# Attention block on one core: another order of the first batch's loads and value tiles, and output products of the last batch per head group

## What is computed

```python
h = jnp.maximum(_layernorm(x, axis=-1), 0.0)
q = heads(h @ Wq + bq); k = heads(h @ Wk + bk); v = heads(h @ Wv + bv)   # 16 heads of 32
scores = jnp.einsum('bhqd,bhkd->bhqk', q, k) * scale
scores = jnp.where(adj[:, None] == 0, -jnp.inf, scores)
attn = jax.nn.softmax(scores, axis=-1)
out = jnp.einsum('bhqk,bhkd->bhqd', attn, v)     # then the heads side by side again
return x + out @ Wo + bo
```

## Time and profile before

| | us |
|---|---|
| three runs: median (lowest to highest) | 1763.75 (1763.15 to 1766.16) |
| the profiled execution, its own time | 1761.98 |
| its span in the profile | 1760.2 |
| PE busy | 1695.4 (96%) |
| DVE busy, ACT busy | 1445.1, 1445.0 (82% each) |
| POOL busy | 139.8 (8%) |
| granted clock of PE, mean | 0.996 |

### The profile page before, as it was taken

The page is one execution under the profiler, slowest core; times in us unless marked ns, Lnnn a source line. Parts: engine busy times, 40 slices in busy tenths (PEclk is TensorE's granted clock), DMA queues, the critical chain, the costliest instruction groups (busy, mean ns, idle before and its releaser), DMA issues.

```text
span 1760.2 us, 27571 instructions
## 1 busy us (share of the span) xinstructions
PE 1695.4 (96%) x8129; PEld 1038.8 (59%) x8256; DVE 1445.1 (82%) x3493; ACT 1445.0 (82%) x3397; POOL 139.8 (8%) x200
## 2 busy tenths in 40 slices
PE   3989999999999999999999999999999999999997
PEld 2646666666666666666665666666566566666643
DVE  5778888888888888888888888888888888888783
...
DMA packets 118677, 175.18 MB, mean 100 GB/s; under 512 B 32384, under 2 KB 34432, under 8 KB 118528
## 3 DMA queue, kind: packets, MB, share of 16 engines
...
...
## 4 chain that ended last, share of the span: by engine, by line
PE 89%; DVE 5%; ACT 3%; issue 1%; DMA 1%; SPq 0%; POOL 0%; POOLq 0%; DVEq 0%; ACTq 0%
PE ps L666 16%; PE psP L590 14%; PE psO L697 14%; PE psP L592 13%; PE psP L591 13%; PE ps L677 12%; PE ps L680 5%; PE ps L638 2%; DVE ps L488 2%; ACT ps L349 1%; PE ps L644 1%; DVE x_tile L416 1%; DVE probs L495 1%; DVE oT_lo L508 1%; ACT probs L379 1%
## 5 line engine op out<-in xcount | busy, mean ns | idle before, releaser
L488 DVE CUSTOM_DVE_ANT_0 ps<-ps,bias_q 128x512 f32<-128x512 f32 x1024 | 710.7, 695 | 237.3 <-PE ps L666 223.4
L349 ACT ACTIVATE ps<-ps,neg_max 128x512 f32<-128x512 f32 x1024 | 680.9, 665 | 76.8 <-DVE neg_max L488 43.7
L379 ACT ACTIVATE probs<-ps 128x512 f32<-128x512 f32 x1024 | 613.2, 599 | 123.9 <-PE ps L677 100.3
L666 PE MATMUL ps<-k_stack,q_stack 96*128 96x512 f32 x1024 | 447.7, 437 | 12.6 <-ACT ps L349 9.4
L677 PE MATMUL ps<-q_stack,k_stack 98*128 98x512 f32 x1024 | 408.6, 400 | 4.0 <-ACT probs L379 3.3
L495 DVE SCALAR_TENSOR_TENSOR probs<-bias_k,probs 128x512 f32<-128x512 bf16 x512 | 365.4, 714 | 13.1 <-ACT probs L379 13.1
L666 PEld LDWEIGHTS ps<-k_stack,q_stack 96*128 96x128 f32 x1024 | 192.4, 188 | 257.8 <-ACT ps L349 108.6
L697 PE MATMUL psO<-probs,v_sb 128*32 128x512 f32 x2048 | 273.2, 605 | 2.7 <-DVE probs L495 1.5
L677 PEld LDWEIGHTS ps<-q_stack,k_stack 98*128 98x128 f32 x1024 | 194.8, 190 | 43.0 <-ACT probs L379 14.7
L349 ACT ACTIVATION_READ_ACCUMULATOR ps<-ps,neg_max 128x1 f32 x1024 | 208.5, 204 | 0.0
L680 PE MATMUL ps<-bias_k,ident_b 128*128 128x512 bf16 x385 | 150.7, 391 | 0.0
...
## 6 DMA issues: line engine op xcount, KB each, us to landing
q_stack<-part_hi SPq DMA_DIRECT2D x512, 64.0 KB, 2.0
k_stack<-part_hi SPq DMA_DIRECT2D x512, 64.0 KB, 2.0
...
```

Source lines behind the costliest of these rows:

```text
L349: nc.scalar.activation(item, item, ACT.Exp, scale=-1.0, bias=neg_max[:, g % 2, col:col + 1], accum_out=exp_sum[:, g % 2, col:col + 1]).the ...
L379: nc.scalar.activation(probs[:, n % P_RING, :], ps2[:, n % 2, :], ACT.Exp, scale=SCALE).then_inc(exp2_done, 1)
L488: nc.vector.tensor_tensor_reduce(bank1(("s", u)), bank1(("s", u)), bias_q[:, qt, :], -SCALE, 3.0e38, ALU.add, ALU.min, neg_max[:, g % 2, c ...
L666: nc.tensor.matmul(bank1(("s", u)), q_stack[0:STACK, g, j, P * qt:P * qt + P], k_stack[0:STACK, g, j, :], start=True, stop=True).then_inc( ...
```

## The change

- **Start.** SP issues x0, x1, then Wv in four quarters, then x2 and x3 (into `y_tile`, which is free), then the three bias vectors as rows into `c_rows`, then Wq, Wk, bo, and Wo after the low part of Wq. The empty block -1 is gone. Wv is staged in `v_sb` and split by quarters (`split_wv`); Wq is split at slots 9 (ACT) and 12 (DVE), Wk at 14 and 15, Wo at 25 and 26.
- **Value tiles.** In block 0 the tiles follow `FIRST_TILES`: v0, v1 and v2 stand in tiles 1 to 3, each waiting only for its own h tile, and v3 in the old place of v0. Tiles 9, 12 and 13 are empty.
- **Biases.** PE turns the three bias vectors in slot 2 of block 0 and ACT copies them to `cols`. PE waits there until they have landed. Before, three transfers of 4-byte elements brought them as columns.
- **Ones.** The two rows of ones in `k_stack` are written by POOL after the four `rstd` of batch 0, no longer by DVE as its first instruction.
- **End.** In blocks 16 and 17 `project_last(g)` makes, for head group g, the 12 products of all four output tiles, into four banks that are held from slot 36 on: g = 0 at slot 36, 1 at slot 42, 2 at slot 52 of block 16, and 3 at slot 0 of block 17. The first waits for the end of the first pass. Tiles 2 and 3 of y of batch 15 lie in `x_tile` and are loaded in slots 48 and 50, with no wait for a store.
- **In every block.** The bfloat16 identity (`ident_b`) is no tile of its own any more, but the upper halves of the float32 one, read with a step of two elements. `exp_sum` has one place in place of two, `ln_sum` is gone (its value goes to `c_all`), and ACT waits at the first exp of each group for the logarithm of the last.

```diff
+FIRST_TILES = [None, ("v", 0), ("v", 1), ("v", 2), ("q", 0), ("k", 0), ("v", 3), ("q", 1), ("k", 1), None, ("q", 2),
+               ("k", 2), None, None, ("q", 3), ("k", 3)]
 QKV_TILES = [x for x in TILES if x[0] != "o"]
+FIRST_QKV_TILES = [x for x in FIRST_TILES if x]
...
+LAST_OUT_AT = {36: 0, 42: 1, 52: 2}
...
-        bq_col = sb("bq_col", [P, NT], F32)
-        bk_col = sb("bk_col", [P, NT], F32)
-        bv_col = sb("bv_col", [P, NT], F32)
+        cols = sb("cols", [P, 3 * NT + 1], F32)
+        bq_col, bk_col, bv_col = (cols[:, NT * i:NT * i + NT] for i in range(3))
+        minus_half = cols[:, 3 * NT:3 * NT + 1]
...
-        ident_b = sb("ident_b", [P, P], BF16)
-        minus_half = sb("minus_half", [P, 1], F32)
+        ident_b = ident[:].bitcast(BF16).rearrange("p (q two) -> p q two", two=2)[:, :, 1]
...
-        exp_sum = sb("exp_sum", [P, 2, 16], F32)
-        ln_sum = sb("ln_sum", [P, 16], F32)
+        exp_sum = sb("exp_sum", [P, 16], F32)
...
+        w_staged = {"q": probs[:, 0:4, :], "k": probs[:, 4:8, :], "v": v_sb[:, 1, :, :], "o": probs[:, 0:4, :]}
+        LAST = B - 1
+        last_turn_bank = RING.index(("c", 3, -1)) % 3
+        last_out = [psP[:, 0, :], psP[:, 1, :]] + [ps1[:, i, :] for i in range(3) if i != last_turn_bank]
...
+        def x_view(b, t):
+            return (y_tile if b == 0 and t >= 2 else x_tile)[:, t % 2, :]
...
+        def y_view(b, t):
+            return (x_tile if b == LAST and t >= 2 else y_tile)[:, t % 2, :]
...
+        def tile_at(k, T):
+
+            if k == 0:
+                return FIRST_TILES[T] and FIRST_TILES[T] + (0,)
+            kind, n = TILES[T]
+            b = k - 2 if kind == "o" else k
+            return (kind, n, b) if have(b) and (kind != "o" or b != LAST) else None
...
+                    if b == LAST and t >= 2:
+                        sp.wait_ge(h_turned, 4 * B)
+                    else:
+                        sp.wait_ge(y_out[t % 2], due(16 * (2 * b + t // 2)))
+                    if b == 0 and t < 2:
+                        sp.wait_ge(h_turned, 4)
+                    sp.dma_start(y_view(b, t), x_rows[bass.ds(row, 1)].rearrange("a p d -> (a p) d")
+                                 ).then_inc(last_y_in[t - 2] if b == LAST and t >= 2 else y_in[t % 2], 16)
...
             def load_weight(n, w):
-                at = 4 * ("qkvo".index(n) % 2)
-                if n in "vo":
-                    sp.wait_ge(w_lo_done, "qkvo".index(n) - 1)
-                sp.dma_start(probs[:, at:at + 4, :], w.rearrange("(t p) d -> p t d", p=P)).then_inc(w_in[n], 16)
+                if n == "o":
+                    sp.wait_ge(w_lo_done["q"], 1)
+                sp.dma_start(w_staged[n], w.rearrange("(t p) d -> p t d", p=P)).then_inc(w_in[n], 16)
...
-                    if u == 1: load_x(k, 2)
-                    if u == 5: load_x(k, 3)
-                    if k == 0 and u == 2: load_weight("v", Wv)
-                    if k == 0 and u == 6: load_weight("o", Wo)
+                    if u == 1 and k > 0: load_x(k, 2)
+                    if u == 5 and k > 0: load_x(k, 3)
...
-                    if u in (7, 11): load_y(k - 2, (u + 1) // 4)
+                    if u in (7, 11) and k - 2 != LAST: load_y(k - 2, (u + 1) // 4)
                     if u in (44, 46): load_y(k - 1, (u - 44) // 2)
+                    if u in (48, 50) and k - 1 == LAST: load_y(LAST, (u - 44) // 2)
...
-            step(-1, 1)
+                        done = tile_at(k, u // 4 - 1) if u >= 4 else tile_at(k - 1, 15)
+                        if done and done[0] in "qk":
+                            load_stack(done[2], QK_ORDER.index(done[:2]))
+
+            load_x(0, 0)
+            load_x(0, 1)
+            for t in range(NT):
+                sp.dma_start(w_staged["v"][:, t, :], Wv.rearrange("(t p) d -> p t d", p=P)[:, t, :]).then_inc(wv_in[t], 16)
+            load_x(0, 2)
+            load_x(0, 3)
+            for i, vector in enumerate((bq, bk, bv)):
+                sp.dma_start(c_rows[NT * i:NT * i + NT, :].bitcast(F32), vector.rearrange("(t p) -> t p", p=P)).then_inc(cols_in, 16)
             load_weight("q", Wq)
             load_weight("k", Wk)
-            with nc.allow_non_contiguous_dma(reason="three bias vectors, once"):
-                sp.dma_start(bq_col[:], bq.rearrange("(t p) -> p t", p=P)).then_inc(small_in, 16)
-                sp.dma_start(bk_col[:], bk.rearrange("(t p) -> p t", p=P)).then_inc(small_in, 16)
-                sp.dma_start(bv_col[:], bv.rearrange("(t p) -> p t", p=P)).then_inc(small_in, 16)
-            sp.dma_start(bo_row[:], bo.rearrange("(a d) -> a d", a=1).to_broadcast([P, D])).then_inc(small_in, 16)
+            sp.dma_start(bo_row[:], bo.rearrange("(a d) -> a d", a=1).to_broadcast([P, D])).then_inc(bo_in, 16)
+            load_weight("o", Wo)
...
-            pool.wait_ge(ident_done, 3)
-            nc.gpsimd.tensor_copy(ident_b[:], ident[:]).then_inc(ident_done, 1)
...
+            for t in range(NT):
+                form_rstd(0, t)
+            pool.wait_ge(rstd_done, 4)
+            nc.gpsimd.memset(k_stack[STACK:STACK + 2].bitcast(F32), 1.0).then_inc(ones_done, 1)
+            pool.wait_ge(ones_done, 1)
+            pool.wait_ge(bo_in, 16)
...
+            def split_wv(t):
+
+                act.wait_ge(wv_in[t], 16)
+                nc.scalar.activation(w_hi["v"][:, t, :], w_staged["v"][:, t, :], ACT.Identity).then_inc(w_hi_done["v"], 1)
...
-                        if u in SPLIT_AT:
-                            split_weight(SPLIT_AT.index(u))
+                        if u in (0, 2):
+                            split_wv(u)
+                            split_wv(u + 1)
+                        if u == 3:
+                            act.wait_ge(cols_turned, 1)
+                            nc.scalar.activation(cols[:, 0:3 * NT], ps2[:, 0, 0:3 * NT], ACT.Identity).then_inc(cols_done, 1)
+                        if u == 9: split_weight("q")
+                        if u == 14: split_weight("k")
                         if u == 16:
-                            act.wait_ge(small_in, 64)
+                            act.wait_ge(cols_done, 1)
+                        if u == 25: split_weight("o")
                         if u == 59:
-                            act.wait_ge(w_lo_done, 4)
+                            act.wait_ge(w_lo_done["k"], 1)
+                            act.wait_ge(w_lo_done["o"], 1)
...
+                        if n % 16 == 0:
+                            act.wait_ge(ln_done, due(4 * b + g))
...
                             act.wait_ge(exp1_done, due(64 * b + n + 1))
-                            act.wait_ge(c_sum_done, due(4 * b + g))
-                            nc.scalar.activation(ln_sum[:], exp_sum[:, g % 2, :], ACT.Ln).then_inc(ln_done, 1)
+                            act.wait_ge(c_lo_done, due(4 * b + g))
+                            nc.scalar.activation(c_all[:], exp_sum[:], ACT.Ln).then_inc(ln_done, 1)
...
-            nc.vector.memset(k_stack[STACK:STACK + 2].bitcast(F32), 1.0)
...
+            def split_wv(t):
+
+                dve.wait_ge(w_hi_done["v"], t + 1)
+                nc.vector.tensor_tensor(w_lo["v"][:, t, :], w_staged["v"][:, t, :], w_hi["v"][:, t, :].bitcast(F32), ALU.subtract
+                                        ).then_inc(w_lo_done["v"], 1)
...
-                        if u in SPLIT_AT:
-                            split_weight(SPLIT_AT.index(u))
+                        if u in (1, 3):
+                            split_wv(u - 1)
+                            split_wv(u)
+                        if u == 3:
+                            ln_stats(0, 2)
+                            ln_stats(0, 3)
+                        if u == 7:
+                            normalise(0, 2)
+                            normalise(0, 3)
+                        if u == 12: split_weight("q")
+                        if u == 15: split_weight("k")
+                        if u == 26: split_weight("o")
                         if u == 16:
-                            dve.wait_ge(small_in, 64)
+                            dve.wait_ge(cols_done, 1)
...
+                        if k - 2 == LAST and T < NT:
+                            done = ("o", T, LAST)
+                        kind, n, b = done or (None, None, None)
+                        if kind == "o":
                             dve.wait_ge(out_done, due(4 * b + n + 1))
                             dve.wait_ge(y_plus_bo, due(4 * b + n + 1))
-                            nc.vector.tensor_tensor(y_tile[:, n % 2, :], psP[:, T % 2, :], y_tile[:, n % 2, :], ALU.add
+                            nc.vector.tensor_tensor(y_view(b, n), last_out[n] if b == LAST else psP[:, T % 2, :], y_view(b, n), ALU.add
...
+                while tile_at(k, T) is None:
+                    k, T = (k, T - 2) if T >= 2 else (k - 1, T + 14)
+                    if k < 0:
+                        return
...
-                    if T == 4:
-
```

(37 more changed lines are left out.)

149 lines of the change are left out of this document (77 added, 72 removed).

## The result

| | before | after |
|---|---|---|
| median, us | 1767.07 (20 runs, 1763.15 to 1771.61) | 1763.54 (20 runs, 1761.27 to 1767.93) |
| ratio to before | | 0.9982, 95% interval 0.9975 to 0.9989 |
| profiled execution, us; its span | 1761.98; 1760.2 | 1763.8; 1761.9 |

The change makes the kernel 3.5 us faster by the medians, 1.9 to 4.4 by the interval. The forecast was a gain of 12.4 and a time of 1751.4, range 1744 to 1759. The profiled execution of before is also a quick one: 5 us under its median, while that of after lies on its own. Their spans are therefore not compared; stretches of them are.

The account below looks back on a forecast made before the run. PE was taken to bound the middle, SP's row of stack issues batch 0. Start 7.2 us plus end 5.2 (11.5 gained, 6.3 paid) gave 12.4 off the 1763.75 median: 1751.4 us, range 1744 to 1759.

Parts of the forecast that it names:

- Loads, first turn, first product of v: Start: bias rows land at about 9.3 us, first h tile is ready then, v0 starts at 9.5.
- The fill on POOL: Start: POOL fills `k_stack` from about 13 us; nobody waits for it before the second pass, so no cost.
- the warning cited beside it: Skill rule: GpSimd contends with DVE instructions having two SBUF inputs; Wq's split could come later by up to the fill's length.
- 24 products less, taken at nothing, bounds 0 and 5.5 of gain: Block 0 after slot 35: v1 and v2 leave, 5.5 us of PE work, gaining nothing because SP's issues cover them.
- The end, gained 11.5: Program's end: only twelve output products remain behind the last value product, which saves 11.5 us.
- The end, paid 6.3: Block 16, slots 36, 42, 52: the other 36 products cost 2.4, 1.7 and 2.2 us, together 6.3.
- Identity with a step of two, in-place logarithm and variance: Every block: these change no length or lie hidden, taken at nothing; other bound for the identity's loads 48 us.
- Rival 3: Second pass, every second score: strided weight load costs as much as float32, unhidden, up to 48 us; chance 0.08.
- Rival 4: Both ends give nothing that lasts, as a later stage waits for something else; 1760 to 1767 us, chance 0.06.
- rival 1: Start gives little: turns and q0 stay cold, or POOL's fill slows the splits; 1756 or 1758 us, chance 0.16.
- Rival 2: Batch 0: SP's issues are not the whole bound, part of the 5.5 us is gained; 1744 to 1747, chance 0.12.
- Baseline: Kernel before: median of the runs shown taken as 1763.75 us, 1.8 above the profiled execution of 1761.98.

Follow-up runs that it names:

- a1_fill_late: The changed kernel, but the ones in `k_stack` are written by DVE in two halves in slots 30 and 34, not by POOL; ratio to before 0.9959.
- c2_after_gap_filled: The changed kernel with 28 useless products put in front of the first score product; ratio to before 0.9956.
- a3_filler: a1_fill_late with three useless products in each of slots 36 to 39 and 48 to 55 of block 0; ratio to before 0.9948.
- a4_old_end: The changed kernel with the end of before: output products in their tiles, last two y tiles handled as before; 1765.32 us beside 1765.49, ratio 0.9996.

## Why the prediction was wrong, step by step

- **Loads, first turn, first product of v**: right. PE waits for the bias rows and starts v0 at 9.68 (forecast 9.5; the loads of the sum are 2.10 MB and not 2.06, which is 0.1 us).
- **The fill on POOL, "nobody waits for it"**: this step failed. Nobody waits for its result, but DVE waits for its end. It was looked at as a thing with readers, not as a thing that shares a way into SBUF with an engine on the chain, and the warning cited beside it was laid against the splits alone. The normalisations ended at 20.94 where about 15.6 was due, 5.3 late; q0 came at 28.50 for 23.7, 4.8 late. q0 itself took 3.9 us to the first stack issue, 3.7 forecast. Of 7.2 us 2.2 were left. With the fill moved, a1_fill_late has its first stack issue at 26.36, 8.3 us earlier than before: the rest of this chain was sound.
- **24 products less, taken at nothing, bounds 0 and 5.5 of gain**: this step failed too, in its sign and in its count. v1, v2 and v3 leave the slots after 35, since v3 moves to the old place of v0: 36 products, 8.3 us (the expectation of c2_after_gap_filled repeats the 24). The row of issues is the bound only while PE's slots keep pace. In the four kernels without v tiles or filler in those slots or in the wait before them it is 67.8 to 68.3 us, in the seven others and before 65.0 to 65.7. Price: 2.7 us; the direct pair, a1_fill_late and a3_filler, which differ in 36 useless products alone, has 68.3 and 65.7. With the stall of the fill that makes 7.7 us of the forecast 7.2 for the start: the x tiles of batch 1 are issued 0.5 us later than before, and a4_old_end shows a start worth nothing. "The products are hidden" was the right reading of the row and the wrong conclusion: here the hidden work also held the clock for what came behind it.
- **The end, gained 11.5**: nearly right, 10.4. In the profile of after the first of the last 12 products ran at 0.43 us, under a low granted clock; where that did not happen the tail is 6.4 us, a gain of 11.8.
- **The end, paid 6.3**: the mechanism was right and the three places too; the size was 7.7, with ACT idle for 2.96, 2.60 and 2.69 us where 2.4, 1.7 and 2.2 were taken. The net is 2.7 for 5.2.
- **Identity with a step of two, in-place logarithm and variance**: right, nothing. Rival 3 is out: 99 ns for 97, and a4_old_end is equal to before. Rival 4 had the time (1760 to 1767) but not the reason: the end does give something, and it is the start whose gain is lost.
- **Sum**: 7.7 of the start and 2.5 of the end are missing from 12.4, which leaves 2.2; measured 3.5 by the medians, 1.9 to 4.4 by the interval.
- **Rivals**: rival 1 came nearest, with the right culprit (POOL's fill, first stack at 32.2 forecast, 32.38 found) and the wrong victim; it still gave 1756, since it let the start keep its 2.4 us. That its 32.2 was met is luck in part: it was added up from five cold quarters and a cold q0, and q0 ran at 0.23 us a product; the stall of the normalisations took the place of these terms, and the cold products of v2 (0.43 us apart from 23.22 on) came only behind it, for a1_fill_late has them at 0.23. Rival 2, the only one that spoke of the products that leave the slots, had them as a gain.
- **Baseline**: the profiled execution was placed 1.8 us under the median of three runs; it is 5.1 under that of twenty. These 3.3 us are no step of the working; without them the time would still be 8.9 from the forecast. The stretch from the first `q_stack` of batch 1 to the end of the first pass, alike in all these kernels, has 1596.5 us in the profile of before and 1597.4 to 1603.0 in the others.

Open: whether the low clock costs through PE's own longer products alone (q3's are the ones that SP waits for) or also through who then waits for whom in the slots before. The rows with 67.8 us and those with 65.2 differ in both. Nor was it tried what a weight split meets that begins during a fill, and not just ahead of it.
